# Table copies spread over more steps, statistics one step later, output weights and zero writes moved, and a bias block of 128 rows

## The reference, cut to what matters

```python
h = concat([token_table[ids], cat_table[ids]], -1)   # cat_table = op, var, const, struct, special
def attn(x):                                         # x = layernorm(h)
    q, k, v = split(x @ W_qkv + b_qkv)
    pq, pk = elu(q) + 1, elu(k) + 1
    kv = einsum('bshd,bshm->bhmd', pk, v)
    z = 1 / (einsum('bshd,bhd->bsh', pq, pk.sum(1)) + 1e-6)
    return einsum('bshd,bhmd,bsh->bshm', pq, kv, z)
h = h + attn(layernorm(h))
x = layernorm(h)
rw = gating(x)                                       # weights of 16 experts per token
q, k, v = [einsum('btc,ech,bte->bth', x, w, rw) for w in (q_proj, k_proj, v_proj)]
a = softmax(causal(q @ k.T / sqrt(128))) @ v
return h + einsum('bth,ehc,bte->btc', a, o_proj, rw)
```

## Time and profile before

| what | value |
|---|---|
| three runs | 1198.89, 1203.84 (median), 1205.63 us |
| the profiled execution's own time | 1205.23 us |
| span of its instructions | 1203.5 us, 1.73 us less than its own time |
| mean granted TensorE clock | 0.949 of full speed |
| busy: PE, PEld, DVE, ACT, POOL | 1033.9, 911.2, 866.8, 606.7, 701.1 us |
| stage 1 with the passage, stage 2, stage 3 | about 0 to 497, 497 to 721, 721 to 1203 us |

### The profile page before, as it was taken

One profiled execution on the slowest core, in us unless ns is written; L12 is line 12 of the kernel. 1 busy time (PEld: TensorE's weight loads), 2 busy tenths in 40 slices (PEclk: granted clock), 3 DMA queues, 4 the chain that ended last, 5 costly groups with the idle time before them and its releaser, 6 DMA issues.

```text
span 1203.5 us, 27580 instructions
## 1 busy us (share of the span) xinstructions
PE 1033.9 (86%) x6831; PEld 911.2 (76%) x6832; DVE 866.8 (72%) x2889; ACT 606.7 (50%) x1569; POOL 701.1 (58%) x924
## 2 busy tenths in 40 slices
PE   0677899988999995289999987999999999999998
PEld 0465677777777774178888876999999999999987
DVE  2445678888888886364444444888888888888988
ACT  2344466666665652144444434555555555555554
POOL 6444566666666656700000006888888888888785
PEclk9878899999999996599999997999999999999999
DMA  6455333333222224567667763323323333333231
GB/s 180 121 175 159 93 99 109 104 108 106 88 89 88 89 80 159 175 206 235 221 223 241 232 198 101 89 87 94 92 89 92 92 87 87 92 92 91 84 90 42
DMA packets 132264, 149.79 MB, mean 124 GB/s; under 512 B 14708, under 2 KB 119650, under 8 KB 132196
## 3 DMA queue, kind: packets, MB, share of 16 engines
q1 hardware_dynamic: 112964, 97.59, 26.1%
q0 software_dynamic: 18080, 50.36, 14.0%
q10 hardware_dynamic: 1152, 1.05, 0.3%
HBM read 83.79 MB, written 78.88 MB: 135 GB/s over the span
## 4 chain that ended last, share of the span: by engine, by line
PE 32%; POOL 26%; issue 19%; DVE 13%; DMA 3%; ACT 3%; POOLq 2%; SPq 1%; another core or an unknown queue 1%; DVEq 0%; ACTq 0%
PE bank L1443 6%; POOL row_y L806 6%; PE bank L1412 6%; PE bank L1414 5%; PE bank L1413 5%; PE bank L1419 5%; POOL x2T L791 4%; POOL qk_neg L791 4%; POOL x2T L793 2%; POOL qk_neg L793 2%; PE bank L1439 2%; POOL x2T L787 2%; POOL qk_neg L787 2%; DVE split_lo L1117 1%; PE bank L1464 1%
## 5 line engine op out<-in xcount | busy, mean ns | idle before, releaser
L1412 PE MATMUL bank<-wo_hi,split_lo 128*128 128x256 f32 x1024 | 304.3, 297 | 12.9 <-DVE qk_e L1349 6.1
L1414 PE MATMUL bank<-wo_hi,split_hi 128*128 128x256 f32 x1024 | 288.7, 282 | 0.0
L1413 PE MATMUL bank<-wo_lo,split_hi 128*128 128x256 f32 x1024 | 288.3, 282 | 0.0
L1412 PEld LDWEIGHTS bank<-wo_hi,split_lo 128*128 128x128 f32 x1024 | 194.0, 189 | 25.4 <-DVE qk_e L1349 12.3
L1413 PEld LDWEIGHTS bank<-wo_lo,split_hi 128*128 128x128 f32 x1024 | 194.1, 190 | 0.0
L1414 PEld LDWEIGHTS bank<-wo_hi,split_hi 128*128 128x128 f32 x1024 | 193.5, 189 | 0.0
L928 ACT ACTIVATE h<-bank,rwo 128x256 f32<-128x256 f32 x256 | 107.6, 472 | 119.3 <-PE bank L1414 113.1
L806 POOL DMA_INDIRECT row_y<-sorted_y,pair_now x128 | 125.4, 980 | 36.7 <-issue 30.1
L705 POOL TENSOR_TENSOR roots<-roots_in,minus_half 128x3 f32<-128x3 f32 x67 | 60.0, 895 | 130.4 <-DVE roots_in L1140 129.4
L799 POOL COPY pair_now<-pair_at 128x2 uint32 (+1 forms) x64 | 11.9, 186 | 208.4 <-SPq L589 208.4
L1349 DVE SCALAR_TENSOR_TENSOR x<-bank,rwo,x 128x256 f32<-128x256 f32 x256 | 109.0, 474 | 20.0 <-PE bank L1414 19.9
(11 more groups left out here) (229 smaller groups left out, 2659.2 us busy)
## 6 DMA issues: line engine op xcount, KB each, us to landing
sorted_y<-row_y SPq DMA_DIRECT2D x36, 384.0 KB, 3.1
sorted_y<-w_attn SPq DMA_DIRECT2D x36, 384.0 KB, 3.1
row_x<-sorted_x SPq DMA_DIRECT2D x72, 128.0 KB, 2.4
h_rows<-h SPq DMA_DIRECT2D x64, 128.0 KB
row_x<-h_rows SPq DMA_DIRECT2D x64, 128.0 KB, 2.1
out_h<-row_x SPq DMA_DIRECT2D x64, 128.0 KB, 1.7
embed_table<-in_L_tok_token_table SPq DMA_DIRECT2D x10, 625.0 KB
embed_table<-in_L_tok_special_table SPq DMA_DIRECT2D x10, 623.0 KB
```

Of the source, the lines that this page charges most:

```text
L1412: pe.matmul(ps, left[1][c], right[0][c], start=(c == 0), stop=False)
L1413: pe.matmul(ps, left[0][c], right[1][c], start=False, stop=False)
L1414: last = pe.matmul(ps, left[0][c], right[0][c], start=False, stop=(c == n - 1))
```

## The change

What it does:

1. The 20 copies for `embed_table` are spread over 14 steps, -7 to 6 (one or two a step), and the four small ones come in step 7.
2. The q, k and v pieces come one a step in steps 7 to 54.
3. DVE takes the layer norm's statistics of tile c + 5, not c + 6, and its bn_aggr stands before `roots_in`.
4. The o_proj pieces are split in steps 8 to 23 of stage 2; SP loads each four steps earlier. The part of stage 2 that is written out before the loop has 24 steps, not 8.
5. The 16 writes of zeros come in steps 20 to 35 of stage 1.
6. Tiles 52 to 55 are scattered two a step in steps 58 and 59, not one a step in steps 58 to 61.
7. The bias block and the block of ones of its product have 128 rows; rows other than 0 and 32 are zero.

```diff
-    COPIES, COPY_FROM = 10, -4
+    COPIES, COPY_FROM, COPY_STEPS = 10, -7, 14
+    WEIGHTS_FROM, DUMMIES_FROM = 7, 20
...
-        bias = sb("bias", [BIAS_ROWS, 3 * C], F32R)
+        bias = sb("bias", [P, 3 * C], F32R)
...
                 at = first + n + 2
-                tiles += [t for t in range(first, first + n) if step == (at + t - first if n == QUAD else at)]
+                late = first + n > B - 12
+                tiles += [t for t in range(first, first + n)
+                          if step == at + ((t - first) * n // QUAD // 2 if late else t - first)]
...
-            if -7 <= i < 0:
-                return range(2 * (i + 7), 2 * (i + 8))
-            n = 14 + i
-            return [n] if 14 <= n < 3 * E else []
+            n = i - WEIGHTS_FROM
+            return [n] if 0 <= n < 3 * E else []
...
-            return 3 * E + i.c + 8 if i.j is None and -8 <= i.c < 8 else None
+            return 3 * E + i.c - 8 if i.j is None and 8 <= i.c < 8 + E else None
...
-            run(eng, step, -8, PAIR_TILES, 8, PAIR_TILES - 9, turn=8)
+            run(eng, step, -8, PAIR_TILES, 8 + E, PAIR_TILES - 9, turn=8)
...
             def step1(i):
-                if 0 <= i.c - COPY_FROM < COPIES:
-                    for skip, at, src in ((N_SMALL, HALF, special_table), (0, 0, token_table)):
+                at = i.c - COPY_FROM
+                if 0 <= at < COPY_STEPS:
+                    for part in range(at * 2 * COPIES // COPY_STEPS, (at + 1) * 2 * COPIES // COPY_STEPS):
+                        skip, column, src = ((N_SMALL, HALF, special_table), (0, 0, token_table))[part % 2]
...
+                if 0 <= i.c - DUMMIES_FROM < E:
+                    n = i.c - DUMMIES_FROM
+                    if n == 0:
+                        sp.wait_ge(consts_ready, N_CONSTS)
+                    sp.dma_start(sorted_x[E * REGION + n * P:E * REGION + (n + 1) * P, :], zeros[:, :]
+                                 ).then_inc(dummies_zeroed, 16)
...
-            sp.wait_ge(consts_ready, N_CONSTS)
-            for n in range(E):
-                sp.dma_start(sorted_x[E * REGION + n * P:E * REGION + (n + 1) * P, :], zeros[:, :]
-                             ).then_inc(dummies_zeroed, 16)
...
-                    if o_weight_at(i) is not None:
-                        load_weight(sp, o_weight_at(i))
+                    early = i.shift(N_RAW)
+                    if i.j is None and o_weight_at(early) is not None:
+                        load_weight(sp, o_weight_at(early))
...
-                x1_tile, attn_tile, phi_tile, ln1_tile = [i.shift(n) for n in (4, 2, 3, 6)]
+                x1_tile, attn_tile, phi_tile, ln1_tile = [i.shift(n) for n in (4, 2, 3, 5)]
...
+                if ln1_tile.inside(B):
+                    after(dve, "ln1_stats", ln1_tile)
+                    dve.bn_aggr(moments[:, ln1_tile.c, 0, :], stats[:, 2 * i.p, :]).then_inc(done["ln1_moments"], 1)
                 row = i.c + 5
...
-                if ln1_tile.inside(B):
-                    after(dve, "ln1_stats", ln1_tile)
-                    dve.bn_aggr(moments[:, ln1_tile.c, 0, :], stats[:, 2 * i.p, :]).then_inc(done["ln1_moments"], 1)
...
-                pe.matmul(ps[:, 0:hi - lo], ones_r[0:BIAS_ROWS, :], bias[:, lo:hi], start=True, stop=False)
+                pe.matmul(ps[:, 0:hi - lo], ones_r[:, :], bias[:, lo:hi], start=True, stop=False)
```

More of the change, by code:

```diff
@@ L127, in build @@
     LAST_STEP = B + 2
-    BIAS_ROWS = 33
+    BIAS_LOW = 32
     OSLOT = E // 2
@@ L221, in build @@
         routing = sb("routing", [P, B, E])
-        bias_raw = routing[0:BIAS_ROWS, :, :].rearrange("p b e -> p (b e)")[:, 0:3 * C]
+        bias_raw = routing[:, :, :].rearrange("p b e -> p (b e)")[:, 0:3 * C]
         pair_w = sb("pair_w", [P, B, 2])
@@ L524, in _ @@
             sp.wait_ge(bias_cleared, 1)
-            for n in (0, BIAS_ROWS - 1):
+            for n in (0, BIAS_LOW):
                 sp.dma_start(bias_raw[n:n + 1, :], b_qkv.unsqueeze(0)).then_inc(inputs_loaded, 16)
@@ L530, in step1 @@
             def step1(i):
-                if 0 <= i.c - COPY_FROM < COPIES:
-                    for skip, at, src in ((N_SMALL, HALF, special_table), (0, 0, token_table)):
+                at = i.c - COPY_FROM
+                if 0 <= at < COPY_STEPS:
+                    for part in range(at * 2 * COPIES // COPY_STEPS, (at + 1) * 2 * COPIES // COPY_STEPS):
+                        skip, column, src = ((N_SMALL, HALF, special_table), (0, 0, token_table))[part % 2]
                         n = -(-src.shape[0] // COPIES)
-                        lo, hi = n * (i.c - COPY_FROM), min(n * (i.c - COPY_FROM + 1), src.shape[0])
-                        sp.dma_start(embed[skip + lo:skip + hi, at:at + HALF], src[lo:hi, :]).then_inc(rows_joined, 16)
-                if i.c == COPY_FROM + COPIES:
+                        lo, hi = n * (part // 2), min(n * (part // 2 + 1), src.shape[0])
+                        sp.dma_start(embed[skip + lo:skip + hi, column:column + HALF], src[lo:hi, :]
+                                     ).then_inc(rows_joined, 16)
+                if at == COPY_STEPS:
                     row = 0
@@ L985, in _ @@
             dve.wait_ge(setup_a, 2)
-            last_row = slice(BIAS_ROWS - 1, BIAS_ROWS)
+            last_row = slice(BIAS_LOW, BIAS_LOW + 1)
             dve.tensor_tensor(bias[last_row, :], bias_raw[last_row, :], bias[last_row, :].bitcast(F32),
```

## The result

| kernel | median, us | range | ratio to before, 95% |
|---|---|---|---|
| before, same chip | 1201.37 | 1198.58 to 1205.63 (4 runs) | |
| changed | 1169.49 | 1166.09 to 1171.71 (4 runs) | 0.9729 [0.9687, 0.9772] |

31.9 us faster, where 34.5 were forecast. The profiled execution has a span of 1170.0 us against 1203.5, with a granted clock of 0.962 against 0.949. The sum came out; two of its terms did not, and it takes the profile to see that.

What follows compares the result with a forecast made beforehand. Early stage 1 was bound by a 9.6 us loop through the small gather, its middle by PE and DVE, stage 2's start by a 5.33 us stall. Terms summed to -34.5 from 1205.2: 1170.7, median 1169 us, range 1158 to 1184.

Steps and rivals of the forecast that it cites:

- to the roots of step 8: Stage 1, up to step 8: later statistics give -23 us (7.0 us a step), the start -4 and -1.
- weights moved to steps 34 to 54: Stage 1: 21 weight pieces enter steps that had none, 0.33 us of DVE each, +7 us (6 to 8).
- bias: Stage 1's bias product: with 128 rows the next weight load overlaps it, -3 us (0 to -6).
- scatters: End of stage 1: POOL's step 60 holds four scatters instead of six, -2.5 us (0 to -3.5).
- zeros: SP's 16 writes moved to stage 1's steps 20 to 35: 0 us (-1 to +1).
- output weights: Stage 2: first split freed of six weights, tile 12 earlier by 8 us, steps 8 to 23 free; -8 (-3 to -10).
- The loop: Early stage 1: roots, small gather, landing, statistics, `roots_in` set 9.6 us a step; spanning two steps, 4.8, no longer binding.
- rival A: Stage 1, steps -1 to 7: POOL's special-row chain takes over at 7.84 us a step; total 1177 us; chance 0.17.
- Rival C: Start of stage 1: the burst of copies slows gather landings above 7 us; 1213 us at 10.3 a step; chance 0.03.
- Rival B: Stage 2: moved output weights cost 5 us where they go, PE near full, DMA at seven tenths; 1174 us; chance 0.12.

Runs made afterwards that it cites:

- the repeat: The changed kernel run once more, unaltered, and profiled again: 1167.26 us, ratio 0.9691 to before.

## Why the prediction came out, term by term

| term | predicted | measured |
|---|---|---|
| to the roots of step 8 (statistics, copies, start) | -28 | -28.6 in the profile, -32.6 in the repeat; statistics alone -25.6 of the median |
| weights moved to steps 34 to 54 | +7 | +5.5 (129.0 - 123.6), with the gain of steps -7 to 6 in the line above |
| bias | -3 | -3.9 alone, [0.9950, 0.9996] |
| scatters | -2.5 | 0 |
| zeros | 0 | not run by itself |
| output weights | -8 | -8.7 at tile 12 (-8.4 in the repeat), then +4.2 to tile 28; 0 of the median |
| sum | -34.5 | -33.5 in the profile, -31.9 and -37.3 of the medians |

*The loop* was read rightly, and so was what comes next. The step is 6.4 to 6.9 us, where 7.0 was taken between 5.87 and 7.84. Both bounds are at work by turns: POOL still waits 18.0 us for special rows, in 8 of 14 gathers; five of these, 9.4 us, lie in steps -1 to 7. So rival A is true of some steps, not of all nine.

*The bias*: The Trainium skill (TensorE: Matmul & The Clock Gate, Part 3) would have it at 0; that 32 rows take as long as 128 stands in the same page's section "Why this matters for your kernels". The trace of the kernel after differs from its rule: the load behind the full block starts 0.07 us after the product, where behind 33 rows it started at 0.40. The measurement decides, for this term.

*Rival C* did not happen; the start up to the roots of step -1 is 4.2 us shorter (44.46 against 48.61), with eight copies in a row. The Trainium skill (DMA: Bandwidth & Descriptors, on arbitration) lets other queues in between packets of a burst. The trace agrees: the small gather that waits for a special one starts 5.65 us after it (78.81 to 84.46), where it was 6.46 us before. While the eight copies were under way it was 7.1 and 6.2 us (6.89 to 13.99, 15.31 to 21.50), against 6.2 and 5.6 of the same two before: the burst did cost up to 0.9 us a gather.

*The output weights* are the step that failed. Its first half was right: tile 12's split starts 22.3 us after the first load (467.40 to 489.68), where 23 were reckoned and 30.8 stood before. Its second half was not. The prediction put it so: "that I count at nothing, and if the cover is gone it is 16 x 0.33 = 5 us". The cover was taken to be PE's work, on engines that are half idle, and the DMA engines' average share. Neither was the limit. What ran short is the queue that issues: SP, which has no row of busy time on the page. Rival B had the place and very nearly the price (5 us; measured 4.2 to tile 28, 5.8 to tile 32), but for a wrong reason, the splits' own time or full engines; with the same splits in the same steps and another queue for the loads the loss is gone. The median shows nothing of the 4 us that are left; they are lost again at the very end, unexplained.

*The scatters* were costed by POOL's longest step. That step was shortened as forecast, but step 62 comes no earlier, so it was not what the end of stage 1 waits for. The wait for centers of the earlier trace rows was taken for the path because it was long.

Two terms were too good: the scatters by 2.5 us, and the output weights, as all that stands behind step 62 is 2.5 us shorter in the profile, not 8 (2.2 in the repeat). This was made up by a start that was 0.6 to 4.6 us better, by steps 34 to 55, which cost 3.8 us instead of 7, by 4.3 us in steps 8 to 34 and by 1.9 us in steps 55 to 62. Of these three stretches the sum had only the 3 us of the bias. In steps 8 to 34, two steps of before, 13 and 21, are 1.0 to 1.5 us longer than their like, and the others are 0.09 us shorter each: 0.055 by the bias, the rest also in the kernel with the statistics alone. The forecast of the total was therefore better than its parts: luck, as far as these go.

What stays open: the stall in step 7 (9.9 us in before, 10.2 in the first profile of the changed kernel, 6.1 in its repeat). It comes in both kernels' first profiles, at the step of the four small copies in the changed one, with a releaser that the profile doesn't know. Six other kernels, whose stage 1 is the same up to there but for the bias block of one, have 6.1 to 7.1 us there. What it is remains unknown. A 4 us error in either direction hides in one profile for that reason, and the ledger's first column should be read with it.

The best kernel of these is the changed one with its output weights in every second step, or from GpSimd's queue: 1157.0 and 1157.9 us, 3.8% below before. The two together, 1156.6, can't be told from either.

## What to carry to other kernels

When a transfer is moved into a steady stage, count the issues and waits of the queue that carries it in one step there, before the engines' busy shares: a queue that must first wait for a buffer holds every load behind it. Look for loops that close through a gather within one step; taking the consumer one step later cost nothing here and was four fifths of the gain. And check a long wait by following what comes after it for two steps: step 60 became 2.5 us shorter, step 61 1.9 us longer, and step 62 came no earlier.

## What the runs showed of the hardware

Copies of 1,250 rows in a row hold the issuing queue. SP's queue in the changed kernel:

```profile
6.24 0.87 SPq L538 DMA_DIRECT2D embed_table<-in_L_tok_special_table  x1
7.16 0.75 SPq L538 DMA_DIRECT2D embed_table<-in_L_tok_token_table  x1
7.95 4.64 SPq L538 DMA_DIRECT2D embed_table<-in_L_tok_special_table  x1
12.63 2.40 SPq L538 DMA_DIRECT2D embed_table<-in_L_tok_token_table  x1
...
23.22 2.24 SPq L538 DMA_DIRECT2D embed_table<-in_L_tok_token_table  x1
```

The first two take 0.75 to 0.87 us, those behind them 2.2 to 4.6, so that the queue is let go only at 25.5 us. To issue the load of a piece takes 0.54 us of POOL, against 0.47 us in the median on SP's queue (0.33 to 1.03), and cost nothing where POOL was idle. And a DMA share of 0.70 in stage 2 (497 to 720 us of the kernel before) was not a limit: 20 us with a share of 0.93 had PE busy throughout.
